# Second attention of a two-layer attention and experts kernel: context loaded before the rows, paired Pool steps, another order of the routing

## The reference, cut to what matters

```python
x = x + _L0_xattn_ref(_layernorm(x), ctx, ctx, mask, wq, wk, wv, wo)   # 16 heads of 16
x = x + _L0_ffn_ref(_layernorm(x), wr, w1, b1, w2, b2)                 # 8 experts, top 2, capacity 560
x = x + _L1_xattn_ref(_layernorm(x), ctx, ctx, bmask)                  # one head of 256, no projections
x = x + _L1_ffn_ref(_layernorm(x), gate_w, w1, w2, w3)                 # 8 experts, top 2, silu gate

def _L1_xattn_ref(query, key, value, mask):
    e = einsum('bid,bjd->bij', query, key) / sqrt(256) - (1 - mask[:, :, None]) * 1e9
    return einsum('bij,bjd->bid', softmax(e), value)
```

## Time and profile before

| | us |
|---|---|
| median of 3 runs (1085.96 to 1093.96) | 1093.72 |
| the profiled execution: its time | 1096.15 |
| its span | 1094.3 |
| last matmul of experts 0 begins | 616.53 |
| first rows of X land, VectorE starts on them | 625.41 |
| first values (L595) begin | 646.57 |
| last attended (L1364) begins | 719.51 |
| first load of a list for experts 1 is issued | 749.55 |
| first matmul of experts 1 begins | 755.80 |

### The profile page before, as it was taken

How to read it: one execution, slowest core, us unless ns; L and a number is a source line. 1 busy time by engine, 2 the same in 40 slices (tenths; PEclk the granted TensorE clock), 3 DMA queues, 4 the chain that set the end, 5 groups by cost and what they waited for, 6 DMA issues and landing times.

```text
span 1094.3 us, 23134 instructions
## 1 busy us (share of the span) xinstructions
PE 953.3 (87%) x8011; PEld 876.2 (80%) x8011; DVE 685.4 (63%) x1937; ACT 544.7 (50%) x1212; POOL 479.0 (44%) x478
## 2 busy tenths in 40 slices
PE   5899999999999478999999567854999999999994
PEld 4778788888887378998999545644999999999993
DVE  6456676576666576666666346773678778776150
ACT  3678878888888445455555223312333343343120
POOL 2023235225213346666666522474446545563222
PEclk8889999999999678999999879975999999999997
DMA  7877787878764277677766776445245434541101
GB/s 191 170 203 189 189 198 202 238 192 213 186 140 108 68 195 184 168 170 168 168 171 146 185 180 165 155 132 200 66 115 140 116 101 107 151 102 40 16 5 21
DMA packets 109670, 160.10 MB, mean 146 GB/s; under 512 B 11360, under 2 KB 98624, under 8 KB 107616
## 3 DMA queue, kind: packets, MB, share of 16 engines
q1 hardware_dynamic: 95600, 140.03, 48.5%
q0 software_dynamic: 13936, 18.33, 8.5%
HBM read 103.32 MB, written 56.96 MB: 146 GB/s over the span
## 4 chain that ended last, share of the span: by engine, by line
PE 42%; DVE 8%; POOL 5%; issue 4%; DMA 3%; ACT 1%; POOLq 0%; DVEq 0%; SPq 0%; ACTq 0%
PE ps L300 36%; DVE HTH L1293 2%; POOL x_scratch L1545 2%; PE ps L647 1%; PE ps L490 1%; DMA CN<-in_ctx_n 1%; POOL xg_scratch L1481 1%; DMA x_scratch<-YY,XG 1%; PE ps L578 1%; POOL rs L1460 1%; DVE WL L915 1%; PE ps L595 1%; POOL HTL L1533 1%; DVE st L1113 1%; ACT GT L816 1%
## 5 line engine op out<-in xcount | busy, mean ns | idle before, releaser
L300 PE MATMUL ps<-XGH,WH 128*128 128x280 f32 (+1 forms) x768 | 225.2, 293 | 9.3 <-ACT GT L816 7.1
L300 PE MATMUL ps<-XGL,WH 128*128 128x280 f32 (+1 forms) x768 | 224.5, 292 | 0.0
L300 PE MATMUL ps<-XGH,WL 128*128 128x280 f32 (+1 forms) x768 | 224.3, 292 | 0.0
L1533 POOL TENSOR_TENSOR HTL<-GT,HTH 128x280 fp32r<-128x280 f32 x128 | 132.6, 1049 | 169.4 <-DVE HTH L1293 169.4
L1165 DVE CUSTOM_DVE_ANT_0 NS<-ps,negm 112x375 f32<-112x375 f32 x256 | 138.0, 545 | 92.9 <-PE ps L406 91.9
L300 PE MATMUL ps<-WH,HTH 128*112 128x256 f32 x568 | 162.3, 286 | 1.5 <-DVE YY L1307 1.5
L300 PEld LDWEIGHTS ps<-XGH,WH 128*128 128x128 f32 x768 | 149.2, 194 | 14.1 <-ACT GT L816 10.3
L300 PE MATMUL ps<-WH,HTL 128*112 128x256 f32 x568 | 159.7, 281 | 0.0
L300 PE MATMUL ps<-WL,HTH 128*112 128x256 f32 x568 | 159.7, 281 | 0.0
L744 ACT ACTIVATE PP<-NS,MN 112x375 f32<-112x375 f32 x256 | 156.5, 612 | 3.9 <-DVE MN L1165 3.3
L300 PEld LDWEIGHTS ps<-XGH,WL 128*128 128x128 f32 x768 | 149.6, 195 | 0.0
(11 more groups left out here) (206 smaller groups left out, 1896.2 us busy)
## 6 DMA issues: line engine op xcount, KB each, us to landing
WG<-in_v SPq DMA_DIRECT2D x48, 512.0 KB, 4.1
KST<-k_scratch SPq DMA_DIRECT2D x48, 376.0 KB, 5.6
WG<-in_w SPq DMA_DIRECT2D x32, 512.0 KB, 4.3
k_scratch<-KHL SPq DMA_DIRECT2D x64, 188.0 KB
CT<-in_ctx_t SPq DMA_DIRECT2D x32, 375.0 KB, 7.1
xg_scratch<-zero SPq DMA_DIRECT2D x8, 1289.8 KB, 10.2
xg_scratch<-zero SPq DMA_DIRECT2D x16, 586.2 KB, 8.9
XG<-xg_scratch SPq DMA_DIRECT2D x14, 586.2 KB, 4.6
```

What stands on the lines that cost most here:

```text
L300: m = e.matmul(out_ap, l, r, start=n == 0, stop=n == len(steps) - 1)
L1533: e.tensor_tensor(HTL[:, f, cols], GT[:, gi % 3, :], HTH[:, f, cols], ALU.subtract).then_inc(hl_pool[layer], 1)
```

## The change

Six edits. SP's order in attention 1: CT2 of batches 0 and 1 and CN of batch 0 are issued ahead of the wait for the rows, and CN of batches 1 to 3 stand between the pieces of X; CT2 and CN move in memory to where no buffer that is still read then lies. Pool's row blocks of the last expert of layer 0 are issued ahead of the low part of chunk 39. Pool takes both inverse roots of a t in one pair of instructions over two columns (one semaphore, rs34), and VectorE's normed4 moves behind mins. Counts, gates and scatters come one or two t sooner. The chunks are 3, 3, 3, 3, 2, 1 and 1 batches. The two chains of a chunk advance in pairs, three steps at a time; from chunk 4 on each chunk is worked off whole.

```diff
 CHUNKS0 = ((0, 4), (4, 4), (8, 4), (12, 3), (15, 1))
-CHUNKS1 = ((0, 3), (3, 3), (6, 3), (9, 3), (12, 3), (15, 1))
+CHUNKS1 = ((0, 3), (3, 3), (6, 3), (9, 3), (12, 2), (14, 1), (15, 1))
+
+LATE1 = 4
...
         Cx = ExitStack()
         XT3 = sb("XT3", [128, 2, 2, S], at=Cx)
-        CT2 = sb("CT2", [128, 4, 2, KEYS], at=Cx)
-        CN = sb("CN", [KC, 4, 3, D], at=Cx)
...
+        sb("past_XG", [128, 10 * RW - 2 * 2 * S - 4 * KEYS - 12 - 6 * S], at=Cx)
+        CT2 = sb("CT2", [128, 4, 2, KEYS], at=Cx)
+        CN = sb("CN", [KC, 4, 3, D], at=Cx)
...
@@ pe_attention1 (act_attention1 is changed in the same way) @@
-            for t in range(B + 15):
-                if 0 <= t - 14 < B and ends_chunk1(t - 14) is not None:
-                    route_counts(ends_chunk1(t - 14))
-                for stage, fn in ((11, route_logits), (10, route_x), (7, values), (6, transposes), (3, scores), (2, queries)):
+            for t in range(B + 12):
+                for stage, fn in ((11, route_logits), (12, late_counts), (10, route_x), (7, values), (13, early_counts),
+                                  (6, transposes), (3, scores), (2, queries)):
...
+        def advance_pairs(routes, n):
+
+            taken = 0
+            for i in range(n):
+                for r in sorted(routes, key=lambda r: (r.order[0], (r.order[1] + i) % 2)):
+                    if r.step(routes):
+                        taken += 1
+                        break
+            return taken
...
@@ dve_attention1 @@
-            for t in range(B + 15):
-                if 0 <= t - 12 < B and ends_chunk1(t - 12) is not None:
-                    c = ends_chunk1(t - 12)
-                    routes += [Route(dve_lists(e, 1, c)), Route(dve_gates1(e, c))]
-                for stage, fn in ((9, normed4), (8, attended), (6, inverse), (4, mins), (1, normed3), (0, stats3)):
+            for t in range(B + 12):
+                late = t - 12 >= CHUNKS1[LATE1][0]
+                if late:
+                    while advance_pairs(routes, 1):
+                        pass
+                if 0 <= t - 12 < B:
+                    route(t - 12)
+                for stage, fn in ((8, attended), (6, inverse), (4, mins), (9, normed4), (1, normed3), (0, stats3)):
+                    if stage == 9 and 0 <= t - 13 < B:
+                        counted(t - 13)
                     if 0 <= t - stage < B:
                         fn(t - stage)
-                        advance(routes, 2, True)
...
+                        advance_pairs(routes, 3)
+                while late and advance_pairs(routes, 1):
+                    pass
+                if late:
+                    counted(t - 12)
+                    while advance_pairs(routes, 1):
+                        pass
+                else:
+                    advance_pairs(routes, 2 if t < B else 12)
...
@@ pool_experts @@
+                last = layer == 0 and ex == E - 1
                 for c in range(5):
                     rows_added(ex, c)
-                    if c < per - 2:
+                    if c < per - 2 and not last:
                         lo(base + per * ex + 10 + c)
+                for c in range(per - 2 if last else 0):
+                    lo(base + per * ex + 10 + c)
...
@@ pool_attention1 @@
-            for t in range(B + 20):
-                if 0 <= t - 1 < B:
-                    pool_rsqrt(e, 4 + (t - 1) % 2, t, var3, rs3)
-                if 0 <= t - 9 < B:
-                    pool_rsqrt(e, 6 + (t - 9) % 2, t - 8, var4, rs4)
-                for b0, nb in CHUNKS1:
-                    if 0 <= t - 15 - b0 - nb < nb:
-                        pool_scatter(e, 1, t - 15 - nb)
+            def roots(t):
+
+                new, old = t - 1 < B, t - 9 >= 0
+                if new:
+                    e.wait_ge(var3, t)
+                if old:
+                    e.wait_ge(var4, t - 8)
+                i = (t - 1) % 2
+                cols = slice(4 + i if new else 6 + i, 7 + i if old else 5 + i, 2)
...
+                e.tensor_scalar(rs[:, cols], st2[:, cols, 1], EPS, None, ALU.add).then_inc(eps, 1)
...
+                e.tensor_tensor(rs[:, cols], rs[:, cols], half, ALU.pow).then_inc(rs34, 1)
+
+            for t in range(1, B + 9):
+                roots(t)
+                for b0, nb in CHUNKS1[:LATE1]:
+                    if 0 <= t - 13 - b0 - nb < nb:
+                        pool_scatter(e, 1, t - 13 - nb)
+            for b in range(B):
+                if b + 13 + next(nb for b0, nb in CHUNKS1 if b0 <= b < b0 + nb) >= B + 9 or b >= CHUNKS1[LATE1][0]:
+                    pool_scatter(e, 1, b)
...
@@ sp_attention1 @@
-            for n in range(5 * E - NY, 5 * E):
-                e.wait_ge(*row_done(0, n))
...
+            e.wait_ge(y_mm[0], 5 * E)
+            context_t(0)
+            context_t(1)
+            context_n(0)
+            for n in range(5 * E - NY, 5 * E):
+                e.wait_ge(*row_done(0, n))
             kept(0)
...
+            context_t(2)
+            kept(1)
+            context_n(1)
+            context_t(3)
+            kept(2)
+            context_n(2)
+            kept(3)
+            context_n(3)
+            for b in range(4, B + 4):
+                if b < B:
+                    context_t(b)
+                if b - 4 >= 4:
+                    context_n(b - 4)
...
```

More of the change, by code:

```diff
@@ L890, in gate_exp, with early_gate, late_gate @@
                 e.activation(v, v, ACT.Exp, scale=-1.0).then_inc(r_exp, 1)
-            for t in range(B + 15):
-                if 0 <= t - 14 < B and ends_chunk1(t - 14) is not None:
-                    gate_exp(ends_chunk1(t - 14))
-                for stage, fn in ((11, logits_out), (10, x4_out), (6, copies), (5, exps), (2, x3_out)):
+            def early_gate(b):
+                if ends_chunk1(b) in range(LATE1):
+                    gate_exp(ends_chunk1(b))
+            def late_gate(b):
+                if ends_chunk1(b) in range(LATE1, len(CHUNKS1)):
+                    gate_exp(ends_chunk1(b))
+            for t in range(B + 12):
+                for stage, fn in ((11, logits_out), (12, late_gate), (10, x4_out), (6, copies), (13, early_gate), (5, exps), (2, x3_out)):
                     if 0 <= t - stage < B:
@@ L1084, in build_kernel, with __init__, step @@
         class Route:
-            def __init__(self, steps):
-                self.steps, self.at = steps, 0
+            def __init__(self, steps, order=(0, 0)):
+                self.steps, self.at, self.order = steps, 0, order
+            def step(self, routes):
+                Chain.at = self.at
+                got = next(self.steps, "end")
+                self.at, Chain.at = Chain.at, Chain.n
+                if got == "end":
+                    routes.remove(self)
+                return got not in ("end", "blocked")
         placed = set()
@@ L1790, in kept, with context_t @@
                 e.dma_start(X[:, b0:b1, :], x_d.ap()[b0 * S:b1 * S, :].rearrange("(b s) d -> s b d", s=S)).then_inc(d_xl[i], 16)
-            kept(0)
-            for t in range(B + 11):
-                if t in (2, 3, 4):
-                    kept(t - 1)
-                b = t
-                if 0 <= b < B:
-                    if b >= 4:
-                        e.wait_ge(sc3, b - 3)
-                    e.dma_start(CT2[:, b % 4, :, :], ctx_t[b].rearrange("(k p) n -> p k n", p=128)).then_inc(d_c2[b % 4], 16)
-                b = t - 5
-                if 0 <= b < B:
-                    if b >= 4:
-                        e.wait_ge(pv3, b - 3)
-                    e.dma_start(CN[:, b % 4, :, :], ctx_n[b].rearrange("(c p) d -> p c d", p=KC)).then_inc(d_cn[b % 4], 16)
-                b = t - 10
-                if 0 <= b < B and b % 4 == 3:
-                    e.wait_ge(res3, b + 1)
-                    e.dma_start(out[b - 3:b + 1].rearrange("b s d -> s b d"), X[:, b - 3:b + 1, :]).then_inc(d_o, 16)
+            def context_t(b):
+                if b >= 4:
+                    e.wait_ge(sc3, b - 3)
+                e.dma_start(CT2[:, b % 4, :, :], ctx_t[b].rearrange("(k p) n -> p k n", p=128)).then_inc(d_c2[b % 4], 16)
@@ new lines, in sp_attention1 @@
+            context_n(1)
[9 more added lines that the diff above has]
+                    context_n(b - 4)
+                last = b - 8
+                if last >= 0 and last % 4 == 3:
+                    e.wait_ge(res3, last + 1)
+                    e.dma_start(out[last - 3:last + 1].rearrange("b s d -> s b d"), X[:, last - 3:last + 1, :]).then_inc(d_o, 16)
@@ L1811, in build_kernel @@
+            e.wait_ge(res3, B)
+            e.dma_start(out[B - 4:B].rearrange("b s d -> s b d"), X[:, B - 4:B, :]).then_inc(d_o, 16)
         block = top.enter_context(nc.Block())
```

50 lines of the change are left out of this document (31 added, 19 removed).

## The result

Over 20 runs of each, the changed kernel takes 1096.77 us (1090.83 to 1102.57) and the kernel before 1092.36 (1085.96 to 1096.90): ratio 1.0038, 95% interval 1.0020 to 1.0055. Forecast were 1.2 us less. On two other chips the same pair gave 1.0004 (0.9981 to 1.0026) and 1.0054 (1.0032 to 1.0075), so the change costs between nothing and 0.7%, most likely about 0.3%. That is within the 1% to which the prediction gave 0.80, with the wrong sign.

What follows compares the result with a forecast made beforehand. CN supply on five DMA engines was taken to bind at the loop's pace; 0.8 us gained at the last CN and 0.4 in the tail gave 1.2 off 1093.7, so 1092.5 us, range 1081 to 1098.

Steps and rivals of the forecast that it cites:

- The bound: Attention 1: CN supply on five DMA engines is a second bound, at the pace of the Pool and VectorE loop, 4.7 us.
- the faster loop at nothing: Pool's pair and normed4 behind mins remove 1.84 us of waiting a turn, costed at nothing because CN supply hides it.
- The sign that the prediction named against it: Turns under 4.3 us while CT2 are being loaded would show the prediction wrong on supply.
- The chain of the beginning: Start of attention 1: weight load waits for Pool's low part, then context, then X; first rows at about 632.7, not 625.4.
- The wait itself: Start of attention 1: first rows come 7 us later, with VectorE, Pool, TensorE and ScalarE standing still behind it.
- The tail: After the last attended: VectorE's late chunks take 25.3 us, list loaded at 29.6 against 30.0 now, gain 0.4 us.
- Rival C: The tail is Pool's: late chunks take 4 us, not 6, list loaded 5 us sooner, 1088 us; chance 0.12.
- rival A: Attention 1's Pool and VectorE loop sets the pace, supply does not: about 11 us gained, 1082 us; chance 0.18.
- the sum for the last CN: Attention 1: 626.0 + 12.5 + 57.6 + 16.0 + 4.9 puts the last CN at 717.0 against 717.8 now.
- the term for the mixed loads: Start of attention 1: X and four CT2 interleaved with CN cost the five engines 12.5 us, between 9.7 and 16.5.
- rival B: Slower: late rows, X and CT2 cost as much mixed as alone (16.5 us), last CN 4.2 us later, 1098; chance 0.20.
- the scatters: Scatters beside the CN loads: about 14 instead of ten by the last CN, at 0.35 us each, 4.9 us.

Runs made afterwards that it cites:

- experiments 1: Changed kernel with its beginning undone (rows first, then context, as before), rest of the change kept: ratio 0.9991 to the kernel before.
- 3: Changed kernel with each CN loaded as two DMAs of 112 and 13 partitions: ratio 0.9842 to the kernel before.
- 6: Kernel before with each CN loaded as two DMAs of 112 and 13 partitions and nothing else: ratio 0.9970 to the kernel before.
- 7: Changed kernel with its beginning undone (rows first) and each CN as two DMAs of 112 and 13 partitions: ratio 0.9864 to the kernel before.
- experiment 11: Changed kernel with CN as two DMAs and Pool's pair undone (four steps a turn), normed4 still behind mins: ratio 0.9876 to the kernel before.
- the repeats: Changed kernel again twice, kernel before once, changed kernel with beginning undone twice; side by side on one chip 1.0054 changed, 1.0012 with beginning undone.
- experiment 12: Changed kernel with CT2 of batch 4 ahead of the largest piece of X, and later each CN ahead of its CT2: ratio 1.0011 to the kernel before.
- experiment 13: Changed kernel with its early scatters two turns later again, as before: ratio 1.0009 to the kernel before.
- experiment 8: Changed kernel with, from batch 8 on, CN of batch b-4 issued ahead of CT2 of batch b: ratio 1.0032 to the kernel before.

## Why the prediction was wrong

**What held.** *The bound*: that five DMA engines' supply of CN and the loop have the same pace is what experiments 1, 3, 6 and 7 show, and the faster loop at nothing is right for the reason given, though what makes it faster is the place of normed4, with or without the pair (experiment 11). The sign that the prediction named against it, turns under 4.3 us while CT2 are loaded, was a bad sign: it came, and meant only that CN had piled up. *The chain of the beginning*: Pool's low part, weight load, context, X, as told. The weight load was issued at +5.6 (forecast 621.8 - 616.85 = +4.95), the rows used at +17.0 (forecast +15.9). The wait itself delayed the attended of batch 0 by 0.5 us and not by 7. *The tail*: list load 30.0 behind the last attended (forecast 29.6, before 30.0), late chunks of 6.0, 5.6 and 5.6 us (forecast 6.2, 5.8, 5.8). Rival C is out, and rival A with it: without the split no form of the loop gained.

**The step that failed** is the sum for the last CN, and in it the term for the mixed loads: "I take 12.5, nearer to the lower end". It gave the last CN at 717.0 - 616.85 = +100.2. The changed kernel begins the last values at +102.4, +102.8 and +104.3, the kernel before at +101.0 and +102.1. Redone with what the first trace of the change has, the weight load issued at +5.6 with the same 4.2 us to land and 12 scatters (4.2 us) instead of 14, the sum leaves 102.4 - 9.8 - 57.6 - 16.0 - 4.2 = 14.8 us for the mixed loads, and 15.2 and 16.7 in the other two traces: not 12.5, but over the 13.3 from which rival B decides and near to the 16.5 of these loads alone. This is a remainder and not a measurement: its other terms are fitted to one trace of before, and the second trace of before begins its last values 1.1 us later.

Rival B, with a chance of 0.20, is what happened. That its time is met so well (4.2 us later, 4.4 between the medians) is luck in part: it had 17 scatters beside the CN, the traces have 12, and the first matmul of experts 1 comes only 2.6 us later in the mean of the traces. That the loss lies in the beginning is likely (the repeats). That it is the price of mixing is argued and not shown: the pause of the five engines does not account for it (experiment 12), TensorE's stop was only moved, never taken away in this kernel, and the scatters (experiment 13) were not settled.

**What was missing.** The sum ended at the last CN and took the rest as fixed. In the first trace of the change the last attended follows its values by 2.8 us instead of 1.7, because TensorE had waited and ran at the lower clock. And the sum took the five engines as one pipe that is always full; the last CN is there when the slowest of the five is, about 2 us behind the others in experiment 12.

## What to carry to other kernels

When two bounds have the same pace, removing either shows little; look for the change that removes the other one and test them two by two. A load of 125 partitions cost this stage 16 us in a loop that was ready for it, and the cure was a second DMA of 13 partitions. In a queue in written order, a load put ahead of the data that starts a stage delays it (rows used 8.4 us later), but what this costs is decided further on: little at the first batch, more where a later load (CT2 of batch 4) now stands behind large ones. And before an experiment is said to have removed a wait, look whether it stands one batch further.

## What the runs showed of the hardware that was not expected

- **A transfer on few engines ends with its slowest.** In the rows of experiment 12 one engine alone moves 24 to 27 GB/s while TensorE waits for the last CN. At 24 GB/s the 75 KB that one of five engines carries take 3.2 us (an estimate, 76,800 bytes by 24 GB/s). The same section of the Trainium skill as above puts such a DMA of SP always on the lowest-numbered engines, so they would be the same five each time; no run here shows which they are, nor why one of them falls behind.
- **SP's issue of a DMA can take ten times as long.** X and CN take 0.3 to 0.5 us to issue where little is outstanding, and 4.09 and 4.57 us in the rows above. By the packet records 2.9 of the 4.1 MB issued since 615.5 had moved when the first of these issues began, and 3.5 of 5.1 MB at the second, so over 1 MB stood ahead of each; that a full queue holds SP there is my reading, not shown. What stands behind them in the list is late by that much before its own transfer begins.
- **TensorE's clock makes a wait for a load longer.** It was 1.00, TensorE was idle from 641.7, and it was 0.58 in the window 644 to 645 and 0.50 up to 654, though TensorE worked again from 650.53. In experiment 8 VectorE waited 4.5 us for counts that TensorE does behind values: TensorE had itself waited 2.53 us for the CN of these values, and then did values and counts at 0.50 (714 to 716):

```profile
716.40 0.18 DVE L1020 SCALAR_TENSOR_TENSOR r_pg<-ps,cst 112x24 f32<-112x24 f32 x1 [4.50 <-PE ps L336]
```
